# An attention and expert block on one core: the first norm in groups of two tiles, the last attention reordered, and another order in the search of the last batch's entries

## The chip, the core and the metric

The kernel runs on one NeuronCore of a Trainium2 chip. TensorE (PE) multiplies matrices and transposes, VectorE (DVE), ScalarE (ACT) and GpSimd (POOL) work on tiles of 128 partitions, SyncE (SP) issues transfers; GpSimd issues the indirect ones. The engines run side by side, each in the order of its own program, and wait for each other by semaphores that count up. The metric is the device time of one execution in microseconds (us). Three runs of the kernel before took 449.43, 449.25 and 447.59 us; the median is 449.25.

## What is computed

The input x is 4 batches of 512 tokens with 512 features; a context holds 64 rows of 128 for each batch.

```python
x = x + jnp.tanh(g_xattn[0]) * _L0_xattn_ref(_layernorm(x, axis=-1), ctx_512, Wq, Wkv_expand, Wout)
x = x + jnp.tanh(g_ffn[0]) * _L0_ffn_ref(_layernorm(x, axis=-1), gate_w, w1, w2, w3, ws1, ws2, ws3)
# attention: 16 heads of 32, causal mask over the 64 context rows, softmax, Wout
# feed-forward: softmax of 8 gate logits, the top 2 experts of each token with their weights,
#   silu(x w1) * (x w3) w2 for them, plus one shared expert of the same shape for every token
```

## The kernel before, in words

Tokens are worked on in 16 tiles of 128, four to a batch. Every matrix is held as two halves of 16 bits, a high one that ScalarE writes (`hi`, L705) and a low one, the rest, that VectorE writes (`lo`, L1061 and L1062), and each product is three matmuls per pair of halves (`product`, L1671). TensorE's transposes (`turn`, L1676) bring tiles into the layout that a product needs; each is followed by its high and its low half.

The program has these stages on TensorE: the first batch's norm, projections, keys and scores; then for each batch b an `iteration` that finishes its attention while the shared expert ("feed-forward") of batch b-1 runs; for the last batch `last_attention` (b = 3, feed-forward of batch f = 2) and `last_feed_forward` (f = 3); and behind them a loop over 39 expert tiles (`step`): 128 rows of tokens are gathered by an indirect transfer, multiplied with the expert's weights, scaled and added to the output. The loop can begin when the list of entries (which token at which place) is known.

The order of the work is written out by hand, engine by engine; nothing schedules it. The places that the change touches:

- Start. VectorE takes `statistics1` of tiles 0 to 3 (L1098), aggregates (L1105), adds epsilon (L1109); GpSimd raises to the power -0.5 (`power1`, L557); VectorE writes the four norms (`first_norm`, L1093). `LN1_GROUPS` says which tiles share one power. TensorE fills its waits with matmuls of the identity that nobody reads (`keep_clock`, L1970).
- Last attention. `head_sum` (L1183, L1186) gives the softmax's sums to GpSimd, which multiplies (L597); TensorE turns the eight probability tiles; `probabilities_lo` writes their low halves; `attend` (L1813) multiplies probabilities and values for the head groups in the order `ATTEND_LAST`, into the banks `mm_bank[g]`; `project_out` (L1824) follows. The banks 0, 1 and 3 of `mm_bank` hold results of the shared expert's `hidden` and of the router until VectorE has read them, so `attend` waits for `g_ready` and `lg_out`.
- Last feed-forward. `router` gives logits; VectorE takes their maximum away (`router_logits`), chooses two experts in some 15 small dependent operations (`router_choose`) and writes a mask; TensorE counts (`count_pairs`, L1752); VectorE turns the counts into places (`last_place`), and writes one-hot rows and blocks (`rows_hot` L1414, `blocks_hot` L1420 and L1422); ScalarE scales each row twice (`send_lists`, L813, 16 operations); TensorE adds them up (`place_lists`, L1767) and finds the entries (`find_entries`, L1777 to L1781); VectorE writes them (L1462). Around them stand the shared expert's `hidden`, `turn_g`, `down` (a product of six matmuls) and VectorE's `hidden` (L1272, L1275) and `base` (L1282, adds a `down` to x). `down(f - 1, 3)` waits for the base of tile 1, `down(f, 0)` for that of tile 2.

In the listing of `bank` names below, bank0 and bank1 are `score_bank`, bank2 and bank3 `turn_bank`, bank4 to bank7 `mm_bank[0]` to `[3]`.

Of the kernel before, what the change touches and what calls it, by code (L numbers as in the profile page):

```python
# [32 lines left out]
P = 128  # L33
# [39 lines left out]
def block_program(nc, x, ctx_rows, gates, wq, wkv, wout, gate_w, experts, out):  # L73
    with ExitStack() as stack:
# [255 lines left out]
        ATTEND_LAST = (0, 2, 3, 1)  # L330

        def down_bank(f, i):
            if f < B - 2:
                return mm_bank[2 + i % 2]
            return (score_bank[1], mm_bank[2], mm_bank[3], mm_bank[2])[i] if f == B - 2 else mm_bank[3 - i % 2]

# [25 lines left out]
        LN1_GROUPS = ((0, PER), (PER, 2 * PER), (2 * PER, NT))  # L362
# [149 lines left out]
        def _(pool):  # L512
# [53 lines left out]
            power1(0)  # L566

# [50 lines left out]
            def iteration(b, prev):  # L618
# [8 lines left out]
                if prev is None:  # L627
                    power1(2)
# [26 lines left out]
            power1(1)  # L655
# [47 lines left out]
        def _(act):  # L703
# [103 lines left out]
            def send_lists():  # L807

                act.wait_ge(sent_step, 3)
                for g in range(2 * PER):  # L810
# [70 lines left out]
            def last_feed_forward(f):  # L881
# [10 lines left out]
                tanh_h(f, 1)  # L892
                tanh_h(f, 2)
                send_lists()
                tanh_h(f, 3)
                got0_high()
                for i in range(PER):
                    turn_hi(c, "g", i)
# [157 lines left out]
        def _(dve):  # L1056
# [32 lines left out]
            def first_norm():  # L1089

                dve.wait_ge(ln1_power, 1)
                for i in range(PER):
                    V.tensor_scalar(xn1[:, i * D:(i + 1) * D], x_tile(i), ln1[:, i, 0:1], ln1[:, i, 2:3],  # L1093
# [33 lines left out]
            def make_x1(b, i):  # L1127
                t = 4 * b + i
                dve.wait_ge(y_mm, t + 1)
                V.scalar_tensor_tensor(out=x_tile(t), in0=mm_bank[i][:, :], scalar=gl[:, 0:1], in1=x_tile(t),  # L1130
# [24 lines left out]
            dve.wait_ge(ld_x0[0], 16)  # L1155
            statistics1(range(2))
            dve.wait_ge(ld_x0[1], 16)
            statistics1(range(2, PER))
            aggregate1(0)
# [168 lines left out]
            def last_attention(b, f):  # L1328
# [6 lines left out]
                turn_lo(b, "x2", 3)  # L1335
                hidden(f, 1)
                head_sum(b, 1)
                turn_lo(b, "g", 0)
                head_sum(b, 2)
                hidden(f, 2)  # L1340
                head_sum(b, 3)
                router_logits(f)
                for i in range(PER):
                    probabilities_lo(b, i)
                hidden(f, 3)
# [139 lines left out]
            def last_feed_forward(f):  # L1485
# [6 lines left out]
                turn_lo(c, "x2", 3)  # L1492
                turn_lo(f, "g", 2)
                turn_lo(f, "g", 3)
                router_logits(f)
# [5 lines left out]
                base(f - 1, 1)  # L1501
# [3 lines left out]
                listed_before()  # L1505
                add_lists()
                turn_lo(c, "g", 0)
                read_entries()
                read_table()
                base(f - 1, 2)  # L1510
# [24 lines left out]
            def iteration(b, prev):  # L1535
# [22 lines left out]
                if prev is None:  # L1558
                    aggregate1(2)
# [11 lines left out]
                if prev is None:  # L1571
                    bias1(2)
# [20 lines left out]
            aggregate1(1)  # L1593
# [524 lines left out]
```

## Time and profile before

| what | value |
|---|---|
| timed runs, us | 449.43, 449.25, 447.59 |
| the profiled execution's own time | 452.13 us |
| its span, first to last instruction | 450.4 us |
| mean granted TensorE clock | 0.986 |
| busy: PE, DVE, ACT, POOL | 414.9, 306.4, 239.3, 229.6 us |
| the chain that ended last, by engine | PE 61%, DVE 19%, POOL 7%, ACT 6%, issue 4% |
| start to the first projection | 14.55 us |
| last attention and last feed-forward | about 195 to 258 us |
| loop over expert tiles | from about 260 us to the end |

All times within the execution are counted from the start of the span. "Busy" is the time in which an engine had an instruction at work; a matmul's end is modelled. The granted clock is a share of full speed: 1.00 is 2.4 GHz, 0.50 is 1.2 GHz. The chain goes back from the last instruction, at each step to what released it.

### The profile page before, as it was taken

What the parts mean: (1) busy time and instruction counts of PE and PEld (TensorE: products, weight loads), DVE (VectorE), ACT (ScalarE), POOL (GpSimd) and SP (SyncE); (2) the same over time, 40 slices, a digit from 0 to 9 for tenths busy, and PEclk for the clock granted to TensorE, in tenths of its full rate; (3) what the DMA queues carried; (4) which work ended last, traced back from release to release, by engine and by line L of the source; (5) the groups of instructions that cost most, each with busy time, mean ns of one, the idle gap of its engine ahead of it and who ended that gap; (6) DMA issues with size and microseconds to landing.
All of it is one profiled execution on the core that took longest, in us unless ns stands there. A gap on an engine that the chain in (4) does not pass through costs nothing.

```text
span 450.4 us, 8467 instructions
## 1 busy us (share of the span) xinstructions
PE 414.9 (92%) x2833; PEld 231.2 (51%) x2834; DVE 306.4 (68%) x663; ACT 239.3 (53%) x432; POOL 229.6 (51%) x206
## 2 busy tenths in 40 slices
PE   7989788999999999998987899999999999999980
PEld 7565445545546554464543455555555555555540
DVE  5989998888688876897869889844444444444430
ACT  2797784676647766855323448734344343434330
POOL 4019435636266762679343217565554646565422
PEclk9999999999999999998998999999999999999997
DMA  8940001706006075084343789575766666666543
GB/s 301 418 169 2 1 12 59 235 3 233 3 1 234 1 262 185 1 304 149 110 143 109 214 285 260 98 138 99 136 106 126 102 130 103 106 126 120 92 62 47
DMA packets 20769, 59.52 MB, mean 132 GB/s; under 512 B 3521, under 2 KB 3521, under 8 KB 20354
## 3 DMA queue, kind: packets, MB, share of 16 engines
q0 software_dynamic: 9504, 20.55, 25.4%
q1 hardware_dynamic: 11234, 38.56, 24.2%
q8 instruction: 19, 0.31, 0.3%
q14 instruction: 12, 0.10, 0.1%
HBM read 35.93 MB, written 23.17 MB: 131 GB/s over the span
## 4 chain that ended last, share of the span: by engine, by line
PE 61%; DVE 19%; POOL 7%; ACT 6%; issue 4%; another core or an unknown queue 1%; DMA 1%; POOLq 0%; DVEq 0%; ACTq 0%
PE bank L1671 46%; PE bank L1676 9%; DVE arena L1062 4%; POOL arena L590 3%; PE bank L1813 3%; POOL GT L615 2%; ACT arena L705 2%; DVE mv L1098 2%; DVE mx L1183 2%; ACT arena L753 1%; DVE xn L1152 1%; POOL ln L557 1%; PE bank L1824 1%; PE bank L1801 1%; DVE arena L1061 1%
## 5 line engine op out<-in xcount | busy, mean ns | idle before, releaser
L1671 PE MATMUL bank<-arena,GT 128*128 x468 | 107.4, 379 | 0.0
L689 POOL DMA_INDIRECT out<-rows,entry x39 | 62.7, 1609 | 65.9 <-issue 33.3
L1671 PE MATMUL bank<-arena,gT 128*128 (+1 forms) x336 | 80.2, 375 | 2.5 <-DVE x_sb L1282 1.3
L1671 PEld LDWEIGHTS bank<-arena,GT 128*128 128x128 f16 x468 | 45.8, 98 | 46.5
L705 ACT ACTIVATE arena<-bank 128x512 f16<-128x512 f32 (+1 forms) x88 | 48.5, 587 | 25.5 <-PE bank L1671 11.4
L666 POOL DMA_INDIRECT rows<-xrows,entry x39 | 38.9, 998 | 33.1 <-DVE entry L1462 11.3
L1062 DVE SCALAR_TENSOR_TENSOR arena<-bank,arena 128x512 f16<-128x512 f32 (+1 forms) x72 | 44.7, 663 | 12.4 <-ACT arena L705 7.5
L1671 PEld LDWEIGHTS bank<-arena,gT 128*128 128x128 f16 x336 | 32.5, 98 | 38.6 <-issue 3.2
L1061 DVE TENSOR_TENSOR gT<-bank,gT 128x256 f16<-128x256 f32 x55 | 23.0, 420 | 42.7 <-ACT gT L705 42.7
L1036 ACT ACTIVATE rows<-bank,weight 128x512 f32<-128x512 f32 x38 | 26.1, 687 | 38.0 <-PE bank L1671 38.0
L1627 DVE SCALAR_TENSOR_TENSOR uu<-th,bank 128x256 f32<-128x256 f32 x39 | 16.4, 421 | 43.4 <-ACT th L1003 42.8
L1671 PE MATMUL bank<-arena,x2T 128*128 128x512 f16 x192 | 45.5, 388 | 0.4 <-DVE x2T L1061 0.4
L1003 ACT ACTIVATE th<-bank 128x256 f32<-128x256 f32 x39 | 15.0, 384 | 56.0 <-PE bank L1671 54.2
L1824 PE MATMUL bank<-arena 128*128 128x512 f16 x192 | 43.7, 380 | 0.0
L1671 PE MATMUL bank<-arena 128*128 128x512 f16 x192 | 43.6, 379 | 0.0
L590 POOL TENSOR_TENSOR arena<-arena,mx 128x1024 f32<-128x1024 f32 x16 | 30.3, 1903 | 14.3 <-DVE mx L1177 7.2
L597 POOL TENSOR_TENSOR arena<-arena,rd 128x1024 f32<-128x1024 f32 x16 | 30.2, 1902 | 12.1 <-DVE rd L1186 11.9
L557 POOL TENSOR_TENSOR ln<-ln,minus_half 128x2 f32<-128x2 f32 (+2 forms) x11 | 9.4, 855 | 42.3 <-DVE ln L1109 42.0
L1676 PE MATMUL bank<-ident,arena 128*128 128x128 f32 x192 | 26.9, 277 | 3.7 <-DVE arena L1062 3.3
L1671 PEld LDWEIGHTS bank<-arena,x2T 128*128 128x128 f16 x192 | 18.6, 99 | 21.7 <-issue 1.9
L1671 PEld LDWEIGHTS bank<-arena 128*128 128x128 f16 x192 | 18.6, 98 | 20.5 <-DVE arena L1061 0.2
L575 POOL DMA_INDIRECT lists<-pair,slot x24 | 23.7, 987 | 10.6 <-issue 6.2
(177 smaller groups left out, 675.2 us busy)
## 6 DMA issues: line engine op xcount, KB each, us to landing
x_sb<-in_experts SPq DMA_DIRECT2D x9, 768.0 KB, 6.1
rows<-in_experts SPq DMA_DIRECT2D x6, 768.0 KB, 6.3
xrows<-xn SPq DMA_DIRECT2D x16, 256.0 KB
out<-x_sb SPq DMA_DIRECT2D x16, 256.0 KB
image<-GT SPq DMA_DIRECT2D x5, 768.0 KB, 4.2
arena<-image SPq DMA_DIRECT2D x10, 384.0 KB, 4.0
x_sb<-in_x SPq DMA_DIRECT2D x1, 2048.0 KB, 16.8
x_sb<-in_x SPq DMA_DIRECT2D x2, 512.0 KB, 4.0
```

Source lines behind the costliest of these rows:

```text
L575: nc.gpsimd.indirect_dma_start(out=lists[:, :], out_offset=bass.IndirectOffsetOnAxis(ap=slot[:, b % 2, k, i:i + 1], axis=0), in_=pair[:, b ...
L590: nc.gpsimd.tensor_tensor(sv, sv, mx[:, i, :].unsqueeze(2).to_broadcast([P, NH, SK]), ALU.subtract).then_inc(sub_ready, 1)
L597: nc.gpsimd.tensor_tensor(sv, sv, rd[:, i, :].unsqueeze(2).to_broadcast([P, NH, SK]), ALU.mult).then_inc(p_ready, 1)
L666: nc.gpsimd.indirect_dma_start(out=G[:, j % RING, :], out_offset=None, in_=xrows[:, :], in_offset=bass.IndirectOffsetOnAxis(ap=entry[:, 0, ...
L689: nc.gpsimd.indirect_dma_start(out=out, out_offset=bass.IndirectOffsetOnAxis(ap=entry[:, 1, j:j + 1], axis=0), in_=Y[:, j % RING, :], in_o ...
L705: return nc.scalar.activation(dst, src, ACT.Copy, scale=scale)
L1036: nc.scalar.activation(Y[:, s, :], e_y[s][:, :], ACT.Copy, scale=weight[:, bass.ds(j, 1)]).then_inc(ey_ready, 1)
L1061: return V.tensor_tensor(dst, src, high, ALU.subtract)
L1062: return V.scalar_tensor_tensor(out=dst, in0=src, scalar=scale, in1=high, op0=ALU.mult, op1=ALU.subtract)
L1671: last = nc.tensor.matmul(dst, a, b, start=n == 0, stop=n == len(steps) - 1)
L1676: last = nc.tensor.transpose(dst[:, c * P:(c + 1) * P], src[:, c * P:(c + 1) * P], ident[:, :])
L1824: last = nc.tensor.matmul(mm_bank[i][:, :], aTv[:, u, g, i * P:(i + 1) * P], woutv[:, v, g, :], start=n == 0 and u + v == 0, stop=n == NG ...
```

## The change

It has three parts. (1) `LN1_GROUPS` begins with two groups of two tiles, so the first norm has two powers on GpSimd, and VectorE aggregates the first pair ahead of the second pair's statistics; the other groups' numbers go up by one. (2) In the last attention the order of the head groups is 2, 3, 0, 1 instead of 0, 2, 3, 1; VectorE takes two softmax sums earlier and the logits and hidden 2 after the eight low halves; TensorE gets two clock-keeping matmuls in front of the attention; the output projection writes its banks in the new order (`out_bank`). (3) In the last feed-forward `down(f - 1, 2)` stands ahead of the pair counts, and `down(f - 1, 3)` behind the entries; the logits are taken ahead of the low halves of two transposes of the shared expert, the second of which goes behind the reading of the old lists; the base of tile 1 moves behind the entries; ScalarE scales two groups of rows ahead of a tanh, and turns one tile ahead of another.

```diff
--- before.py
+++ after.py
@@ -327,13 +327,17 @@
 
-        ATTEND_LAST = (0, 2, 3, 1)
+        ATTEND_LAST = (2, 3, 0, 1)
 
         def down_bank(f, i):
...
 
+        def out_bank(b, i):
+
+            return mm_bank[ATTEND_LAST[i] if isinstance(b, int) and b == B - 1 else i]
+
         MIX_FIRST = (("q", 0), ("q", 1), ("v", 0), ("q", 2), ("p", 0), ("v", 1), ("q", 3), ("p", 1), ("v", 2),
@@ -359,7 +363,7 @@
 
-        LN1_GROUPS = ((0, PER), (PER, 2 * PER), (2 * PER, NT))
+        LN1_GROUPS = ((0, 2), (2, PER), (PER, 2 * PER), (2 * PER, NT))
 
@@ -564,6 +568,7 @@
             power1(0)
+            power1(1)
 
             def scatter_pairs(b, choices=(0, 1)):
@@ -625,7 +630,7 @@
                 if prev is None:
-                    power1(2)
+                    power1(3)
                 else:
@@ -652,7 +657,7 @@
 
-            power1(1)
+            power1(2)
             softmax_mask(0)
@@ -804,10 +809,10 @@
 
-            def send_lists():
+            def send_lists(g0, g1):
 
                 act.wait_ge(sent_step, 3)
-                for g in range(2 * PER):
+                for g in range(g0, g1):
                     act.wait_ge(row_hot, g + 1)
@@ -890,11 +895,13 @@
                 tanh_h(f, 1)
+                send_lists(0, 2)
                 tanh_h(f, 2)
-                send_lists()
+                send_lists(2, 2 * PER)
+                got0_high()
+                turn_hi(c, "g", 0)
                 tanh_h(f, 3)
-                got0_high()
-                for i in range(PER):
+                for i in range(1, PER):
                     turn_hi(c, "g", i)
...
             def probabilities_hi(b, i):
@@ -1088,8 +1095,8 @@
             def first_norm():
 
-                dve.wait_ge(ln1_power, 1)
                 for i in range(PER):
+                    dve.wait_ge(ln1_power, 1 + i // 2)
                     V.tensor_scalar(xn1[:, i * D:(i + 1) * D], x_tile(i), ln1[:, i, 0:1], ln1[:, i, 2:3],
@@ -1127,7 +1134,7 @@
             def make_x1(b, i):
...
                 dve.wait_ge(y_mm, t + 1)
-                V.scalar_tensor_tensor(out=x_tile(t), in0=mm_bank[i][:, :], scalar=gl[:, 0:1], in1=x_tile(t),
+                V.scalar_tensor_tensor(out=x_tile(t), in0=out_bank(b, i)[:, :], scalar=gl[:, 0:1], in1=x_tile(t),
                                        op0=ALU.mult, op1=ALU.add).then_inc(x1_ready, 1)
...
             def statistics2(b, i):
@@ -1152,11 +1159,10 @@
 
-            dve.wait_ge(ld_x0[0], 16)
-            statistics1(range(2))
-            dve.wait_ge(ld_x0[1], 16)
-            statistics1(range(2, PER))
-            aggregate1(0)
+            for n in range(2):
+                dve.wait_ge(ld_x0[n], 16)
+                statistics1(range(2 * n, 2 * n + 2))
+                aggregate1(n)
             own_block()
@@ -1333,15 +1339,15 @@
                 turn_lo(b, "x2", 3)
+                head_sum(b, 1)
                 hidden(f, 1)
-                head_sum(b, 1)
+                head_sum(b, 2)
                 turn_lo(b, "g", 0)
-                head_sum(b, 2)
-                hidden(f, 2)
                 head_sum(b, 3)
-                router_logits(f)
                 for i in range(PER):
                     probabilities_lo(b, i)
+                router_logits(f)
+                hidden(f, 2)
                 hidden(f, 3)
@@ -1490,23 +1496,23 @@
                 turn_lo(c, "x2", 3)
+                router_logits(f)
                 turn_lo(f, "g", 2)
-                turn_lo(f, "g", 3)
-                router_logits(f)
                 router_choose(f, 0)
...
                 hidden(f, 1)
-                base(f - 1, 1)
                 rows_hot()
...
                 listed_before()
+                turn_lo(f, "g", 3)
                 add_lists()
...
                 read_table()
+                base(f - 1, 1)
                 base(f - 1, 2)
@@ -1556,7 +1562,7 @@
                 if prev is None:
-                    aggregate1(2)
+                    aggregate1(3)
                 for g in range(NG):
@@ -1569,7 +1575,7 @@
                 if prev is None:
-                    bias1(2)
+                    bias1(3)
                 head_max(b + 1, 1)
@@ -1590,9 +1596,9 @@
             statistics1(range(PER + 2, 2 * PER))
-            aggregate1(1)
+            aggregate1(2)
             project_lo(0, 1)
-            bias1(1)
+            bias1(2)
             keys_lo()
@@ -1821,7 +1827,7 @@
                     for u, v in ((0, 0), (0, 1), (1, 0)):
-                        last = nc.tensor.matmul(mm_bank[i][:, :], aTv[:, u, g, i * P:(i + 1) * P], woutv[:, v, g, :],
+                        last = nc.tensor.matmul(out_bank(b, i)[:, :], aTv[:, u, g, i * P:(i + 1) * P], woutv[:, v, g, :],
                                                 start=n == 0 and u + v == 0, stop=n == NG - 1 and u == 1)
@@ -1879,13 +1885,13 @@
                     turn_probabilities(b, i)
-                pe.wait_ge(g_ready, 4 * f + 3)
+                keep_clock(2, mm_bank[2])
                 split_done(b, "p", 2 * PER - 1)
...
                         pe.wait_ge(lg_out, f + 1)
-                    if g == 1:
-                        pe.wait_ge(g_ready, 4 * f + 4)
+                    if g < 2:
+                        pe.wait_ge(g_ready, 4 * f + 3 + g)
                     attend(b, g).then_inc(a_mm, 1)
@@ -1908,15 +1914,15 @@
                 hidden(f, 1)
+                down(f - 1, 2)
                 count_pairs(f)
                 hidden(f, 2)
-                down(f - 1, 2)
+                turn_g(f, 0)
                 hidden(f, 3)
+                place_lists()
+                turn_g(f, 1)
+                find_entries()
                 down(f - 1, 3)
-                place_lists()
-                turn_g(f, 0)
-                find_entries()
-                turn_g(f, 1)
                 down(f, 0)
...
```

VectorE at the start of the program; `mv` and `ln1` are the statistics and what the norm needs of them, `own` belongs to the expert lists. Before:

```order
L1098 BN_STATS mv<-x_sb 128x6 [waits ld_x0_0]
L1098 BN_STATS mv<-x_sb 128x6
L1098 BN_STATS mv<-x_sb 128x6 [waits ld_x0_1]
L1098 BN_STATS mv<-x_sb 128x6
L1105 BN_AGGR ln1<-mv 128x2 [waits ln1_step]
L1105 BN_AGGR ln1<-mv 128x2 x3
L1109 TENSOR_SCALAR ln1<-ln1 128x4 [waits ln1_step]
L1067 TENSOR_REDUCE own<-before_e 128x1 [waits consts]
L1068 CAST along16<-along 128x128
L1070 SCALAR_TENSOR_TENSOR own<-own,down_no 128x1 [waits own_step]
L1093 TENSOR_SCALAR arena<-x_sb,ln1 128x512 [waits ln1_power]
```

And now (the last row stands for the four norms, each with its own wait):

```order
L1105 BN_STATS mv<-x_sb 128x6 [waits ld_x0_0]
L1105 BN_STATS mv<-x_sb 128x6
L1112 BN_AGGR ln1<-mv 128x2 [waits ln1_step]
L1112 BN_AGGR ln1<-mv 128x2
L1116 TENSOR_SCALAR ln1<-ln1 128x2 [waits ln1_step]
L1105 BN_STATS mv<-x_sb 128x6 [waits ld_x0_1]
L1105 BN_STATS mv<-x_sb 128x6
L1112 BN_AGGR ln1<-mv 128x2 [waits ln1_step]
L1112 BN_AGGR ln1<-mv 128x2
L1116 TENSOR_SCALAR ln1<-ln1 128x2 [waits ln1_step]
L1100 TENSOR_SCALAR arena<-x_sb,ln1 128x512 [waits ln1_power] x4
```

The second pair's statistics now stand behind the first pair's scaling, and each pair has its own.

TensorE between the last probability transposes and the output projection of the last attention; rows with `ident,arena` are transposes, those of 32x512 the attention products, bank4 to bank7 are `mm_bank[0]` to `[3]`. Before:

```order
L1676 MATMUL bank2<-ident,arena 128x128 [waits turned_lo]
L1676 MATMUL bank2<-ident,arena 128x128 x3
L1813 MATMUL bank4<-arena 32x512 [waits turned_lo,g_ready]
L1813 MATMUL bank4<-arena 32x512 x11
L1813 MATMUL bank6<-arena 32x512 x12
L1813 MATMUL bank7<-arena 32x512 [waits lg_out]
L1813 MATMUL bank7<-arena 32x512 x11
L1813 MATMUL bank5<-arena 32x512 [waits g_ready]
L1813 MATMUL bank5<-arena 32x512 x11
```

And now:

```order
L1682 MATMUL bank2<-ident,arena 128x128 [waits turned_lo]
L1682 MATMUL bank2<-ident,arena 128x128 x3
L1976 MATMUL bank6<-ident 128x128 x2
L1819 MATMUL bank6<-arena 32x512 [waits turned_lo]
L1819 MATMUL bank6<-arena 32x512 x11
L1819 MATMUL bank7<-arena 32x512 [waits lg_out]
L1819 MATMUL bank7<-arena 32x512 x11
L1819 MATMUL bank4<-arena 32x512 [waits g_ready]
L1819 MATMUL bank4<-arena 32x512 x11
L1819 MATMUL bank5<-arena 32x512 [waits g_ready]
L1819 MATMUL bank5<-arena 32x512 x11
```

Two matmuls of the identity stand ahead of the attention; the bank that waited for nothing new comes first, those of hidden 2 and 3 last.

TensorE in the last feed-forward, from hidden 1 (bank5) to the first down product of the last batch; `mask16` are the pair counts, bank4 and bank5 with `x2T` hidden 2 and 3, `rows` the list products, `pick` the entries. Before:

```order
L1671 MATMUL bank5<-arena,x2T 128x512 [waits turned_lo]
...
L1752 MATMUL bank0<-mask16,earlier 128x32 [waits mask_ready]
...
L1671 MATMUL bank4<-arena,x2T 128x512 [waits g_ready,turned_lo]
...
L1671 MATMUL bank7<-arena,gT 128x512 [waits lg_out,turned_lo]
...
L1671 MATMUL bank5<-arena,x2T 128x512 [waits g_ready,turned_lo]
...
L1671 MATMUL bank6<-arena,gT 128x512 [waits base_ready,turned_lo]
...
L1767 MATMUL bank1<-rows 128x384 [waits sends,hots,base_ready]
L1767 MATMUL bank1<-rows 128x384 [waits sends,hots] x7
L1676 MATMUL bank2<-ident,gg 128x128 [waits turned_lo,g_ready]
...
L1781 MATMUL bank0<-pick,got 128x39 [waits got_ready]
...
L1676 MATMUL bank3<-ident,gg 128x128 [waits turned_lo,g_ready]
...
L1671 MATMUL bank7<-arena,gT 128x512 [waits base_ready,turned_lo]
```

And now:

```order
L1677 MATMUL bank5<-arena,x2T 128x512 [waits turned_lo]
...
L1677 MATMUL bank7<-arena,gT 128x512 [waits lg_out,turned_lo]
...
L1758 MATMUL bank0<-mask16,earlier 128x32 [waits mask_ready]
...
L1677 MATMUL bank4<-arena,x2T 128x512 [waits g_ready,turned_lo]
...
L1682 MATMUL bank2<-ident,gg 128x128 [waits turned_lo,g_ready]
...
L1677 MATMUL bank5<-arena,x2T 128x512 [waits g_ready,turned_lo]
...
L1773 MATMUL bank1<-rows 128x384 [waits sends,hots,base_ready]
L1773 MATMUL bank1<-rows 128x384 [waits sends,hots] x7
L1682 MATMUL bank3<-ident,gg 128x128 [waits turned_lo,g_ready]
...
L1787 MATMUL bank0<-pick,got 128x39 [waits got_ready]
...
L1677 MATMUL bank6<-arena,gT 128x512 [waits base_ready,turned_lo]
...
L1677 MATMUL bank7<-arena,gT 128x512 [waits base_ready,turned_lo]
```

The product into bank7 moved ahead of the counts, that into bank6 from ahead of the list products to behind the entries, and one transpose of `gg` to ahead of hidden 3.

## Rows read from the trace of the kernel before

**Rows 1.** The page: the span.
```profile
span 450.4 us, 8467 instructions
```
**Rows 2.** The chain that ended last: start us, us, what.
```profile
260.49 3.88 PE bank L1671 x18
```
**Rows 3.** Timeline of the start: start us, us, engine, line, what [idle before <-releaser].
```profile
2.38 6.03 PE L1970 MATMUL bank<-ident 128*128 128x128 f32 x28 [2.38 <-POOL earlier L523]
...
4.43 2.54 DVE L1098 BATCH_NORM_STATS2 mv<-x_sb 128x6 f32<-128x512 f32 x4 [4.43 <-DMA x_sb<-in_x]
...
7.12 0.38 DVE L1105 BATCH_NORM_AGGREGATE ln<-mv 128x2 f32<-128x6 f32 x4
7.53 0.17 DVE L1109 TENSOR_SCALAR ln<-ln 128x4 f32<-128x4 f32 x1
...
7.86 1.05 POOL L557 TENSOR_TENSOR ln<-ln,minus_half 128x4 f32<-128x4 f32 x1 [2.58 <-DVE ln L1109]
...
8.95 1.91 DVE L1093 TENSOR_SCALAR arena<-x_sb,ln 128x512 f32<-128x512 f32 x4 [0.85 <-POOL ln L557]
...
14.55 5.35 PE L1671 MATMUL bank<-arena 128*128 128x512 f16 x24
```
**Rows 4.** Timeline, a norm of two tiles in the last attention.
```profile
219.82 0.69 DVE L1098 BATCH_NORM_STATS2 mv<-x_sb 128x6 f32<-128x512 f32 x1
...
221.20 0.72 POOL L557 TENSOR_TENSOR ln<-ln,minus_half 128x2 f32<-128x2 f32 x1 [3.52 <-DVE ln L1109]
```
**Rows 5.** Timeline of the last attention, up to its products.
```profile
199.93 5.74 POOL L597 TENSOR_TENSOR arena<-arena,rd 128x1024 f32<-128x1024 f32 x3 [1.01 <-DVE rd L1186]
...
203.65 3.41 PE L1676 MATMUL bank<-ident,arena 128*128 128x128 f32 x24
...
203.87 4.86 DVE L1062 SCALAR_TENSOR_TENSOR arena<-bank,arena 128x512 f16<-128x512 f32 x8
204.28 3.41 ACT L705 ACTIVATE arena<-bank 128x512 f16<-128x512 f32 x6
```
**Rows 6.** Attention products: the timeline; stretches: us, PE busy (x), others, PEclk.
```profile
57.55 2.77 PE L1813 MATMUL bank<-arena 64*32 64x512 f16 x48 [1.73 <-DVE arena L1062]
...
208.88 4.46 PE L1813 MATMUL bank<-arena 64*32 64x512 f16 x48 [1.83 <-DVE arena L1062]
...
208.88:213.34 4.46, 4.46 (x49) 1.97 (x50) 2.15 (x5) 1.79 (x3) 4.30 (x6) 0.62 0.58 180
...
171.75:174.45 2.70, 2.70 (x51) 1.14 (x52) 1.95 (x3) 2.38 (x4) 0.00 (x0) 1.00 0.61 170
```
**Rows 7.** Timeline of the last feed-forward, around the router's logits.
```profile
233.86 0.65 PE L1671 MATMUL bank<-gate_s,x2T 128*128 128x8 f16 x20
...
234.96 0.66 ACT L705 ACTIVATE gT<-bank 128x256 f16<-128x256 f32 x2 [3.76 <-remote]
...
236.05 0.18 DVE L1198 TENSOR_REDUCE m<-bank 128x4 f32<-128x32 f32 x1
```
**Rows 8.** Timeline, TensorE around the mask.
```profile
235.02 2.75 PE L1671 MATMUL bank<-arena,x2T 128*128 128x512 f16 x12
...
240.31 0.21 PE L1752 MATMUL bank<-mask,earlier 128*128 128x32 f16 x1 [2.54 <-DVE mask L1236]
...
240.55 4.18 PE L1671 MATMUL bank<-arena,x2T 128*128 128x512 f16 x12
```
**Rows 9.** Timeline of the search, up to the loop's first product.
```profile
243.02 0.74 DVE L1282 SCALAR_TENSOR_TENSOR x_sb<-bank,gl,x_sb 128x512 f32<-128x512 f32 x1
...
245.04 4.77 ACT L813 ACTIVATE rows<-rows,sent 128x128 f16<-128x128 f16 x16
...
249.74 1.46 PE L1767 MATMUL bank<-rows 128*128 128x384 f16 x8
...
252.22 0.19 DVE L1462 TENSOR_SCALAR entry<-bank 128x39 int32<-128x39 f32 x1
...
260.32 2.75 PE L1671 MATMUL bank<-arena,GT 128*128 x12
```

## The prediction

> **What bounds the kernel now.** I read the chain that ended last first, then the timelines of the three places that the change touches, then a table of stretches for the granted clock. From 260.49 us on the chain is TensorE alone, one expert tile after another [rows 2]; no edit touches that loop, so the time changes only by how much earlier or later it begins. Before it the three places bound differently.
>
> At the start VectorE sets the end: 28 clock-keeping matmuls end at 8.41, the four statistics are done at 6.97, aggregation and scaling at 7.70, GpSimd's power ends at 8.91, and only then VectorE writes the norms, without a pause until the first projection at 14.55 [rows 3]. In the last attention VectorE is full too: eight low halves of the turned probabilities from 203.87 to 208.73, and TensorE, which ended its transposes at 207.06, waits 1.83 us for them [rows 5, 6]. In the last feed-forward TensorE waits 2.54 us for the router's mask (VectorE's chain of small operations) before the pair counts [rows 8]; then the search for the entries runs over VectorE, ScalarE and TensorE in turn and ends at 252.22 + 0.19; the loop's first product starts at 260.32 [rows 9].
>
> Two things in this execution need care. First, the granted clock. After the wait of 1.83 us the attention's 48 matmuls take 4.46 us with the mean clock at 0.62, where the same 48 take 2.70 at 1.00 [rows 6]: 1.76 us lost to the lower level (1.2 GHz instead of 2.4). After the wait of 2.54 the twelve matmuls of a hidden product take 4.18 instead of 2.75: 1.43 us [rows 8]. A wait of 1.73 elsewhere cost nothing: 48 matmuls in 2.77 [rows 6]. Second, ScalarE stands still for 3.76 us before 234.96 with "remote" as its releaser, although the transposes that it needed had been issued well before [rows 7]; the router's logits on VectorE, queued behind it, start at 236.05. Without it they would follow TensorE's router products. Those had issued 20 of 24 matmuls in 0.65 us from 233.86 [rows 7], so the whole lasts 0.78 and the logits start some 0.13 later, at 234.77: 1.28 us earlier. The mask's wait then shrinks to 1.7 us, for TensorE is earlier too (0.47 us, its own pause at 234.5), and a wait of 1.73 kept the clock. An execution without the standstill is thus shorter by 1.28 + 1.43 = 2.71.
>
> **The time that the sum starts from.** The profiled execution took 452.13 us, 1.73 around its span of 450.40 [rows 1]. Minus 2.71 that is 449.42; the timed runs are 449.43, 449.25 and 447.59. So I take the timed runs to have no standstill, two of them one fall of the clock, and the third none: it is 1.66 to 1.84 below, and the fall costs 1.76. Start: 449.42.
>
> **Part 1, the first norm in groups of two.** The first pair's statistics end 1.27 after 4.43, the aggregation for two and its scaling end at about 6.3, the second pair's statistics at 7.5, its scaling at 8.1 and the three small "own block" operations at 8.45. From last statistics to the start of a power for two columns it is 0.69 us (220.51 to 221.20), and the power lasts 0.72 [rows 4], against 1.05 for four [rows 3]; the first power then ends at 7.1 and the second at 8.9, before norm 2 needs it at 9.35. Norm 0 starts at 8.42 instead of 8.95: -0.53. TensorE's next two keeping matmuls now follow the 28 directly and end at 9.0, when norm 0 is there. Behind it VectorE is full until 14.55, so the gain goes through. Bounds: 0 (TensorE's dummies or a weight split is late) and -0.9 (the whole pause in front of norm 0). Added: one power (0.72, GpSimd idle), one more aggregation group on VectorE (0.3, in its pause).
>
> **Part 2, the last attention.** Sum 1 moves ahead of hidden 1, and the logits and hidden 2 behind the eight low halves; the first of these can start at 202.8 instead of 203.87. But from the third on they follow ScalarE's high halves, six in 3.41 us from 204.28 [rows 5], and TensorE's transposes, which come behind a hidden product that does not move. The eighth low half of VectorE then starts at 207.98 at best and ends at 208.6: -0.13. The softmax's third multiply on GpSimd ends 0.5 earlier [rows 5], which nobody waits for. The logits and hidden 2 and 3 (0.4 + 0.8 + 0.8) now stand between 208.5 and 210.5, inside the attention products: product 3 of the new order 2, 3, 0, 1 needs hidden 2 at 211.0 and gets it at 209.6. The two keeping matmuls (0.6) run in the wait and leave 1.1 us idle in place of 1.83; with 1.73 kept, the clock stays: -1.76. Bounds: 0 (it falls all the same) and -1.76. I take -1.76.
>
> The Trainium skill ("TensorE: Matmul & The Clock Gate", "What's actually happening") says that what watches TensorE runs free and does not restart with a kernel, so that the same wait may be followed by a fall in one execution and not in another. The trace cannot show it, but the third timed run agrees; by that rule the medians before hold either 447.6 or 449.3, and the gain of this part is 1.76 or nothing.
>
> **Part 3, the search.** Three effects. (a) The base of tile 1 (0.74, [rows 9]) leaves VectorE's path in front of the hot rows, a low half (0.34) enters it before the lists are added, and ScalarE's 16 scaled copies, 4.77 us in one run [rows 9], can start with the first hot rows: entries 0.43 earlier. (b) That base and TensorE's down product of tile 3 (half of a hidden product's 2.75, 1.3 issued) now stand behind the entries. There both engines have no pause to speak of: 8.1 us from the entries' write to the first loop product [rows 9]. All but 0.2 of the 1.3 is new there: +1.10. Sum of (a) and (b): +0.67. Bounds: -0.43 (all of (b) hidden) and +1.3. The down product of tile 2, put in the mask's wait, is hidden there (1.3 into 1.7), but what it filled before it no longer fills. (c) That is the clock. Before, hidden 3 and two down products kept TensorE full until the eight list products, which ran back to back in 1.46 us [rows 9]. Now hidden 3 ends at 244.9, and the list products come one by one behind ScalarE's copies until 247.3; then TensorE waits for the fourth low half, the entries and the moved base. Its work from 244.9 to 250.2 is 1.46 + 0.4 + 0.4 + 0.2 = 2.5 us, 2.9 idle in pieces. After 1.83 idle in one piece the clock fell, so I expect a fall here. A fall costs 1.43 to 1.76 where TensorE is always busy; some 0.4 of slack are left, I take +1.2. Bounds 0 and +1.76.
>
> **Sum.** 449.42 - 0.53 - 0.13 - 1.76 + 0.67 + 1.2 = 448.87; forecast 448.9, no change that can be told from 449.25. What a measurement here can tell is about 0.5%, 2.2 us.
>
> **Rivals.**
> - R1, no fall in the emptied stretch. For it: TensorE never idles 1.8 in one piece there. Against: half of the stretch is idle. 448.87 - 1.2 = 447.7. Chance 0.18.
> - R2, the standstill at 231.2 belongs to the program and every run has it. For it: its releaser is a real event, and the work of all engines stops on it. Against: the sum above meets the timed runs only without it. Then the logits move ahead of the two low halves that wait for ScalarE and gain 0.77, the second fall (1.43) goes, since the wait shrinks by the product put in it, and the new fall comes: part 3 gives 0.67 - 0.77 - 1.43 + 1.2 = -0.33, and the timed 449.25 becomes 449.25 - 0.53 - 0.13 - 1.76 - 0.33 = 446.5. Chance 0.24. [...]
> - R3, slower: the clock falls in the last attention in spite of two keeping matmuls (0.6 of 1.8 us filled, and the low level lasts through all four products), while part 3 costs its full price. 449.42 - 0.53 - 0.13 + 0.67 + 1.2 = 450.6, and 451.2 if part 1 is hidden. It decides as soon as TensorE's remaining idle of 1.1 us counts as the 1.83 did. Chance 0.12.
> - That the change does not move what it says is excluded for part 1 and 3 by the order of instructions; others, 0.04.
>
> **Range and chances.** Forecast 0.42 (447.9 to 449.7), R1 0.18 (446.8 to 448.4), R2 0.24 (445.4 to 447.4), R3 0.12 (449.9 to 452). 446.0 to 450.7 leaves out half of R3's upper part and the lower third of R2. Faster by over 0.5% (below 447.0): 0.20 of R2, 0.06 of R1, 0.02 else: 0.28. Slower (above 451.5): 0.04 of R3, 0.02 else: 0.06. The rest, 0.66.
>
> **What would show it.** Norm 0 near 8.4 and the first projection near 14.0. The attention's 48 matmuls in 2.7 to 2.8 at a clock of 1.00, with the eighth low half ending near where it did, counted from hidden 3. No ScalarE wait for "remote" of 3.8 us (else R2). TensorE waiting 0.6 for the mask. From the entries' write to the first loop product 9.0 us or more, with the clock down in between; if it is under 8.3 at full clock, part 3 was priced wrongly.

## The result, and the profile after

The changed kernel takes 450.16 us, the median of 20 runs (447.47 to 452.46); the kernel before, run beside it, 448.33 (447.38 to 450.63, 20 runs). The ratio is 1.0039, 95% interval 1.0024 to 1.0054: slower, by less than the 0.5% that the prediction called no change. The forecast of 448.9 had the sign wrong; 450.16 lies inside the range and outside the likeliest case's own (447.9 to 449.7).

The single times stand at levels. For the changed kernel the mean granted clock of the run is given in brackets, and it goes with them:

| kernel | us (mean clock where given), number of runs |
|---|---|
| before, 20 runs | 447.4 to 447.6, 10; 449.1 to 449.5, 9; 450.63, 1 |
| changed, 20 runs | 447.5 (0.993), 1; 449.0 to 449.4 (0.988 to 0.99), 6; 450.1 to 450.4 (0.984), 7; 451.7 to 452.5 (0.98), 6 |

The profiled execution of the changed kernel took 451.73, 1.73 around its span. The start, in the timeline, answers to [rows 3]:

```profile
6.23 1.28 DVE L1105 BATCH_NORM_STATS2 mv<-x_sb 128x6 f32<-128x512 f32 x2
...
8.41 1.91 DVE L1100 TENSOR_SCALAR arena<-x_sb,ln 128x512 f32<-128x512 f32 x4
9.00 1.11 PE L1682 MATMUL bank<-ident,arena 128*128 128x128 f32 x8 [1.04 <-DVE arena L1100]
...
14.00 1.25 PE L1677 MATMUL bank<-arena 128*128 128x512 f16 x5
```

Norm 0 starts at 8.41 and the first projection at 14.00, as forecast. Attention products and the search answer to [rows 6] and [rows 9]:

```profile
57.02 4.15 PE L1819 MATMUL bank<-arena 64*32 64x512 f16 x48 [1.73 <-DVE arena L1069]
...
207.62 0.61 PE L1976 MATMUL bank<-ident 128*128 128x128 f32 x4
209.51 0.83 PE L1819 MATMUL bank<-arena 64*32 64x512 f16 x12 [1.29 <-DVE arena L1069]
...
242.33 3.60 ACT L818 ACTIVATE rows<-rows,sent 128x128 f16<-128x128 f16 x12
...
245.49 0.32 PE L1773 MATMUL bank<-rows 128*128 128x384 f16 x1 [0.26 <-ACT rows L818]
...
246.07 0.32 PE L1773 MATMUL bank<-rows 128*128 128x384 f16 x1 [0.26 <-ACT rows L818]
...
247.14 0.41 PE L1682 MATMUL bank<-ident,gg 128*128 128x128 f32 x2 [0.75 <-DVE gT L1068]
...
247.94 0.20 DVE L1468 TENSOR_SCALAR entry<-bank 128x39 int32<-128x39 f32 x1
...
248.26 1.39 DVE L1288 SCALAR_TENSOR_TENSOR x_sb<-bank,gl,x_sb 128x512 f32<-128x512 f32 x2
...
249.14 5.28 PE L1677 MATMUL bank<-arena,gT 128*128 128x512 f16 x12 [1.24 <-DVE x_sb L1288]
...
254.53 1.46 PE L1677 MATMUL bank<-arena,gT 128*128 128x512 f16 x6
...
259.74 2.54 PE L1677 MATMUL bank<-arena,GT 128*128 x11
```

Stretches of the same trace (us, busy time and count of TensorE, its weight loads, VectorE, ScalarE and GpSimd, then granted clock, DMA share, GB/s):

```profile
56.43:59.84 3.41, 2.83 (x28) 1.07 (x32) 2.63 (x12) 1.62 (x3) 1.20 (x1) 0.50 0.00 0
...
209.51:212.28 2.77, 2.77 (x49) 1.18 (x50) 2.67 (x8) 2.02 (x4) 2.77 (x4) 1.00 0.64 162
...
243.46:249.14 5.68, 2.87 (x16) 1.16 (x15) 5.35 (x26) 3.71 (x13) 0.08 (x1) 0.86 0.73 294
247.58:254.41 6.83, 5.59 (x18) 2.24 (x17) 4.38 (x15) 0.38 (x1) 2.90 (x3) 0.50 0.59 174
```

Three things are to be seen. The last attention keeps its clock (2.77 us at 1.00, where [rows 6] has 4.46 at 0.62). The first attention, whose code the change leaves alone, has lost it behind a wait of 1.73 us: 4.15 us, while the same wait in [rows 6] was followed by 2.77. And in the search TensorE is busy for only 2.87 us of the 5.68 from the first list product to the two down products; after these short pieces of work, with waits of 0.26, 0.75 and 1.24 us between them, the clock is down for 6.83 us, so that the twelve matmuls of the two down products take 5.28 (2.75 at full clock in e5, below). From the entries to the loop's first product it is 259.74 - 247.94 = 11.80 us (8.10 in [rows 9]). The mask's wait and ScalarE's:

```profile
231.11 0.38 ACT L710 ACTIVATE gT<-bank 128x256 f16<-128x256 f32 x1 [0.96 <-PE bank L1682]
...
237.85 0.19 PE L1758 MATMUL bank<-mask,earlier 128*128 128x32 f16 x1 [0.39 <-DVE mask L1242]
```

No standstill of 3.76 us [rows 7], and 0.39 for the mask in place of 2.54 [rows 8]; the prediction's sign was 0.6.

### The profile page after: what moved, and what is told of

It reads as the page before. It is cut to its first block, busy times and chain, and to the rows that moved or that the text cites. A ratio compares the mean times of both kernels' runs of the same rounds, so it can differ in the third digit from the quotient of the medians.

```text
span 450.0 us, 8478 instructions
## 1 busy us (share of the span) xinstructions
PE 415.2 (92%) x2837; PEld 230.4 (51%) x2838; DVE 306.5 (68%) x664; ACT 239.4 (53%) x432; POOL 228.0 (51%) x207
## 4 chain that ended last, share of the span: by engine, by line
PE 65%; DVE 15%; ACT 6%; POOL 6%; issue 4%; DMA 1%; POOLq 0%; DVEq 0%; ACTq 0%
PE bank L1677 50%; PE bank L1682 10%; DVE arena L1069 4%; PE bank L1819 3%; POOL GT L620 2%; ACT arena L710 2%; POOL arena L595 2%; DVE mv L1105 2%; ACT arena L758 1%; DVE xn L1159 1%; PE bank L1830 1%; PE bank L1807 1%; ACT rows L818 1%; POOL ln L561 1%; DVE arena L1068 1%
## 5 line engine op out<-in xcount | busy, mean ns | idle before, releaser
L694 POOL DMA_INDIRECT out<-rows,entry x39 | 61.5, 1578 | 69.4 <-issue 34.2
L1677 PE MATMUL bank<-arena,gT 128*128 (+1 forms) x336 | 82.6, 384 | 2.6 <-DVE x_sb L1288 1.6
L1677 PE MATMUL bank<-arena,x2T 128*128 128x512 f16 x192 | 44.0, 379 | 0.4 <-DVE x2T L1068 0.4
L1068 DVE TENSOR_TENSOR GT<-bank,GT 128x512 f16<-128x512 f32 x39 | 26.9, 690 | 2.8 <-ACT GT L710 0.8
```

What stands on the lines that cost most here:

```text
L694: nc.gpsimd.indirect_dma_start(out=out, out_offset=bass.IndirectOffsetOnAxis(ap=entry[:, 1, j:j + 1], axis=0), in_=Y[:, j % RING, :], in_o ...
L1068: return V.tensor_tensor(dst, src, high, ALU.subtract)
L1677: last = nc.tensor.matmul(dst, a, b, start=n == 0, stop=n == len(steps) - 1)
```

## The experiments

Five jobs; in each the kernels run in turns with the kernel before on one chip. "Keeping matmuls" are `keep_clock`, each about 0.3 us, on a bank that nobody uses then. "Kept" is a place whose wait has them. The prices below are taken inside one job, or between jobs 2 and 3, which ran on one chip; any other difference across jobs is rougher.

**Job 1, the parts alone** (before here: 447.7, 13 runs; 449.3, 15; 450.71, 1). e1 is the norm's edits, e2 the last attention's with its two keeping matmuls, e3 the search's, e4 e1 and e2 together: each a part of the diff above, word for word.

> Only the first norm in groups of two (part 1). All theories: norm 0 at 8.4 and first projection at 14.0 as in the changed kernel, 0.53 us less where TensorE's clock does the same. Theory S (the search order and the clock falls in its emptied stretch are the whole loss): the runs lie 0.5 below those of the kernel before, at about 447.0 and 448.8, median near 448. Rival N (the shift by 0.55 us is what brings the clock down in the first attention, 57 us, where the changed kernel's profile has it): a level 1.4 higher appears, median 449 or more.

> Only the last attention's new order and the two clock-keeping matmuls (part 2). Theory S: the upper of the two levels of the kernel before (449.3 against 447.5) thins out or goes, because the fall in the last attention does, and both are 0.1 lower: most runs near 447.4, median 447.4 to 447.8. Rival A (the keeping matmuls don't hold the clock in other executions, or the fall of the timed runs is elsewhere, at the mask's wait): two levels as before, median 448.3 to 449.2.

> Only the search's new order (part 3). Theory S: no run under 448.0 (447.4 + 0.67), most at 450 to 452: one or two falls of 1.3 to 2.7 us on top, median about 451, slower than before by 2 to 3 us. Rivals N and A: the search is worth what its order gives, 0.67 at most, median 448.5 to 449.3. The profile should show 11 to 12 us from the entries' write to the loop's first product and the clock at 0.50 in it.

> Parts 1 and 2 with the search as before. Theory S: 0.66 below the kernel before at equal clock, and the last attention's fall gone: most runs at 446.8, some one fall higher (448.5), median 446.8 to 447.5, faster than before by 1 us or more. Rival N: a third of the runs or more at 448.2 and above because of the first attention; median 448.5. Rival A: two levels at 446.9 and 448.6 in equal numbers.

Measured: e1 447.10 (447.0 in 7 runs, 448.5 to 448.8 in 4, one 450.15). e2 448.79 (447.2 in 4, 449.1 in 8). e3 452.43, ratio 1.0081 (1.0052 to 1.0110), no run under 449.99. e4 448.31, ratio 0.9977 (0.9959 to 0.9995): 447.0 in 5, 448.4 in 7. So the search is the loss, and parts 1 and 2 are a gain of 0.7 us between the lower levels (447.0 against 447.7). In the profile of e3's fastest run (449.99) it is 257.94 - 247.38 = 10.56 us from the entries to the loop, not the 11 to 12 expected, with one fall of the clock. The timeline, then the stretch:

```profile
248.58 4.09 PE L1673 MATMUL bank<-arena,gT 128*128 128x512 f16 x12 [1.24 <-DVE x_sb L1284]
...
247.94:251.35 3.41, 2.77 (x7) 1.02 (x8) 2.25 (x6) 0.00 (x0) 2.24 (x3) 0.50 0.61 192
```

But the second level did not go with the last attention's fall: rival A's two levels came in e2 and e4, though not from the mask's wait that it named. The profiles of both show where the fall was, at the first attention. Since e2 has it without part 1, rival N (part 1's shift brings it) is not needed. Of e4:

```profile
57.00 4.26 PE L1817 MATMUL bank<-arena 64*32 64x512 f16 x48 [1.73 <-DVE arena L1067]
...
209.56 2.77 PE L1817 MATMUL bank<-arena 64*32 64x512 f16 x48 [1.29 <-DVE arena L1067]
```

**Job 2.** e5 keeps the clock in the search's emptied stretch:

```
...
                                             start=g == 0, stop=g == 2 * PER - 1)
+                    if 4 <= g < 7:
+                        keep_clock(1, score_bank[0])
...
+                pe.wait_ge(pos_out, B)
                 place_lists()
+                keep_clock(3, score_bank[0])
                 turn_g(f, 1)
                 find_entries()
+                keep_clock(4, score_bank[1])
                 down(f - 1, 3)
```

e6 undoes the moved work:

```
                 hidden(f, 1)
+                base(f - 1, 1)
                 rows_hot()
...
                 read_table()
-                base(f - 1, 1)
...
                 hidden(f, 3)
+                down(f - 1, 3)
                 place_lists()
                 turn_g(f, 1)
                 find_entries()
-                down(f - 1, 3)
```

e7 is e4, and e8 the kernel before, with four keeping matmuls in the first attention (e8: four in the last attention too):

```
+if prev is None:
+    pe.wait_ge(v_lo, 1)
+    keep_clock(4, mm_bank[0])
 split_done(b, "p", 2 * PER - 1)
```

> The changed kernel with ten more clock-keeping matmuls in the stretch that its search empties: one behind each of list products 5 to 7, three ahead of the turn of g 1, four (1.2 us) ahead of the down product that waits for the base. Theory S (the falls in that stretch are what makes the changed kernel slower; the moved work costs about 0.6 at full clock): the levels with mean clock 0.984 and 0.980 go, what is left are runs at 447.5 and, with one fall elsewhere, 449.1; median 447.5 to 449.1, at or under the kernel before. Rival W (the moved base and down product themselves cost it, the clock only follows): median stays at 450 or above.

> The changed kernel with two things put back: down product 3 of the batch before stands ahead of the list products again, and its base 1 on VectorE ahead of the hot rows. The rest of the search's new order stays. Theory S: the emptied stretch is full again; the copies of ScalarE still start early, so the entries come about as early as in the kernel before or a little earlier. Levels 446.6 to 447.0 and one fall higher (448.4 to 448.7); median 447 to 448.5. Rival P (what hurts is the single copies and list products, which still arrive one by one): the clock still falls there, median 449 or more.

> Parts 1 and 2 (search as before) and four clock-keeping matmuls (1.2 us) in the wait of 1.73 us in front of the first attention's products at 57 us. Theory F (the second level of the runs is one fall of the clock at that wait): the level at 448.4 goes, all runs at 446.9 to 447.1. Rival M (the fall of the other runs is in the wait for the router's mask, 1.7 us at 235 us, or anywhere else): two levels as in the kernel with parts 1 and 2, 447.0 and 448.4, median between.

> The kernel before with four clock-keeping matmuls (1.2 us) in each of two waits, in front of the first attention's products (1.73 us) and of the last attention's (1.83 us), nothing else changed. Theory F: all runs at 447.4 to 447.7, the level at 449.3 is gone. Rival M: two levels, 447.5 and 449.3, as before. If only some of the upper level goes, both waits and a third place share the falls.

Measured: e5 447.78, ratio 0.9988 (0.9969 to 1.0006): nine runs at 447.6 to 448.3, three at 449.1 to 449.7. Only ten idle-time matmuls and one wait (`pos_out`) away from the changed kernel, it is 2.4 us below the first comparison's 450.16, and the ratio to the kernel before is 0.9988 against 1.0039; W falls. From its entries to the loop it is 257.33 - 248.11 = 9.22 us at full clock.

```profile
248.11 0.20 DVE L1468 TENSOR_SCALAR entry<-bank 128x39 int32<-128x39 f32 x1
...
249.31 2.75 PE L1677 MATMUL bank<-arena,gT 128*128 128x512 f16 x12 [0.25 <-DVE x_sb L1288]
...
257.33 2.75 PE L1677 MATMUL bank<-arena,GT 128*128 x12
```

e7 446.86, ratio 0.9961 (0.9948 to 0.9975), and e8 447.54, ratio 0.9974 (0.9959 to 0.9990): 12 runs each, one level each. Theory F holds: the two levels of the kernel before are falls of the clock at these two waits. A third level, 450.4 to 451.2, holds 12 of its 138 runs outside job 4; it is gone too, and its height fits both falls in one run, but no profile shows it. The wait for the mask, 1.69 us, stays unfilled in e7 and e8, and no run of theirs stands on an upper level. e6 451.65 (six runs, 451.4 to 453.4, ratio 1.0073): S is missed, and P's "449 or more" came by a wait that neither named. I had left the low half of g 3 where the change put it, behind the hot rows, and the down product needs it.

```profile
248.15 2.27 PE L1677 MATMUL bank<-arena,gT 128*128 128x512 f16 x6 [4.09 <-DVE gT L1068]
```

**Job 3.** e9 is the changed kernel with the four of e7. e10 is e6 with them and with `turn_lo(f, "g", 3)` ahead of VectorE's hidden 1. e11 is e7 without part 2's `keep_clock(2, mm_bank[2])`. e12 is e1 with the keeping matmuls of e8.

> The changed kernel with four clock-keeping matmuls in the wait of 1.73 us in front of the first attention's products, nothing in the search. Theory S: what is left are the falls in the emptied stretch, of 3.4 us (cost 1.5) or 6.8 us (cost 2.7); levels 447.5 (rare), 449.0 and 450.2, the one at 451.9 gone; median 449.0 to 450.2, slower than the kernel with parts 1 and 2 and the same four by 2 to 3 us. Rival: the four also cure the rest, median 447.6.

> The kernel with down product 3 and base 1 put back, with the low half of g 3 put back too (behind the router's choice, ahead of hidden 1), since the down product needs it, and with the four keeping matmuls in the first attention. ScalarE's early copies and down product 2 in the mask's wait remain of the search's new order. Theory L (the loss of the kernel without this was that low half behind the hot rows, for which TensorE stood 4.09 us): the list products follow the down product at once, no wait over 1 us; one level at 446.3 to 447.0, at or below 446.86 of parts 1 and 2 with the four. Rival P (single copies and list products are the trouble): 448 or more, clock down near 247.

> Parts 1 and 2 with the four keeping matmuls in the first attention, but without part 2's own two in the last attention (the wait there is 1.8 us again). If those two keep the clock (theory F): a second level at about 448.5 comes back, in a quarter to a half of the runs. Rival (part 2's order alone, or chance, held it): one level at 446.9 as with them.

> Part 1 and four keeping matmuls in each of the two attention waits; the last attention's order and the search as in the kernel before. It prices part 2's order alone against 446.86 (parts 1 and 2 with the keeping matmuls): by my sum the order is worth 0.13, so 447.0; if it is worth nothing, 446.9; if it is worth more, 447.2. And against the keeping matmuls alone (447.54) it prices part 1: 0.53 gives 447.0, one level.

Measured: e9 450.20: 447.69 once, 448.7 to 449.4 three times, 450.1 to 450.6 (clock 0.984) eight times; the level at 452 is gone. So the changed kernel's levels are, by their height and clock: no fall, a short or a long one in the stretch, and the long one with the first attention's. Profiles show the long one (e9) and the last (the changed kernel). e10 448.18: L is right that the wait of 4.09 goes (the longest left is 1.24, not under 1), the four runs at full clock lie at 447.0 to 447.4, but in eight the time is 447.9 to 449.3, and the profile of one has the clock down for 6.83 us, as P had it: it takes full clock to judge an order. e11 446.97: nine runs at 446.7 to 447.0, three at 448.4 to 448.9, so without part 2's two matmuls a second level is back in 3 of 12. That these are falls in the last attention is inferred: e11's profile is of a run without one, and only [rows 6] shows that fall. e12 447.05, one level.

**Job 4** ran on a chip where the kernel before takes 448.97 in 5 runs and 450.4 to 453.7 in 12. e13 is e5 with the four of e7; e14 is e10 with a keeping matmul behind list products 6 and 7 and four behind the entries; e15 is e7 again.

> The changed kernel with the clock kept everywhere: four keeping matmuls in the first attention's wait, ten in the search's emptied stretch, the last attention's two as they are. Theory S: one level, at 447.6 to 447.8, no run above 448.3; minus 446.86 it is what the search's new order costs at full clock, 0.8. Rival W (part of the loss of the changed kernel is neither the order nor the clock): a second level or a median above 448.3.

> The kernel with the down product, base 1 and low half of g 3 put back and the first attention kept, with six keeping matmuls more in the search: one behind each of list products 6 and 7, four ahead of the down product that waits for the base. Theory S: one level at 446.9 to 447.3 (its lower level without them was 447.2), all of the upper one was the clock. If ScalarE's early copies and down product 2 in the mask's wait are worth anything, it is below 446.86; I expect not.

> Parts 1 and 2 with the four keeping matmuls in the first attention, once more, beside the two others on the same chip: one level, 446.8 to 447.1, and the fastest of the three.

Measured: e13 448.25 and e14 447.72, six runs and one level each; e15 449.14, six runs at 448.1 and six at 449.9, ratio 0.9970 (0.9949 to 0.9991). The expected numbers are missed by 0.4 to 2.0 us; the reason is in all three profiles. Of e15:

```profile
232.32 0.66 ACT L710 ACTIVATE gT<-bank 128x256 f16<-128x256 f32 x2 [3.74 <-remote]
...
237.66 0.19 PE L1756 MATMUL bank<-mask,earlier 128*128 128x32 f16 x1 [2.53 <-DVE mask L1240]
```

This is the standstill of [rows 7] with the mask's wait of [rows 8]. No profile of the other jobs has it. So it goes with this chip or this job, which one job cannot tell apart, and it is in the timed runs too: 448.97 is 1.5 above the 447.5 of other jobs, the prediction's price of it 1.28. Which chip the profile of the kernel before came from is not on record.

**Job 5**, on a chip without it (before 447.5 in 11 runs, 449.1 in 13, 450.5 in 2). e16 is e7 with `keep_clock(4, score_bank[0])` ahead of `count_pairs(f)` in the last feed-forward, behind a wait for `pos_out`; e17 is e14, e18 the changed kernel.

> Parts 1 and 2, four keeping matmuls in the first attention, and four more (1.2 us) in TensorE's wait for the router's mask (1.7 us, or 2.5 where ScalarE stands still for 3.8 us). If the second level of the same kernel without the last four, 1.8 above the first on the chip with the standstill, is a fall at that wait: one level here on either kind of chip, 446.9 without the standstill, 448.1 with it. Rival: it comes from elsewhere, two levels 1.8 apart remain on a chip with the standstill.

> The kernel e14 again, beside the others. With the standstill 447.7 as before, and 0.2 to 0.5 faster than the one with the mask's wait kept, since the router's logits come ahead of the low half that waits for ScalarE; without it 447.0 to 447.2, not faster than it.

> The changed kernel as it is. Without the standstill: levels 447.6, 449.1, 450.2, 452, median 450.2, beside 448.3 to 449.2 of the kernel before. With the standstill, where the search's new order wins some of it back: 448.3 at full clock, mostly 449.8 to 451.5, median near the 450.5 that the kernel before has there.

Measured: e16 446.62, ratio 0.9956 (0.9939 to 0.9973), one level; e17 446.97, one level; e18 451.62, ratio 1.0046 (1.0023 to 1.0069), seven of its twelve runs at 451.6 to 452.6. For e18 the expected median, 450.2, is missed by 1.4: more of its runs stand on the highest level than in the first comparison (7 of 12, there 6 of 20). That the mask's wait makes e15's second level is not shown, since e16 did not meet the standstill and e15's profile has no fall; for it speak [rows 8], where the clock fell behind that wait of 2.54, and e13 and e14, which wait 0.49 and 0.48 there and have no second level. How the changed kernel does on that chip stays open too. e16 has the lowest median of the study, 2.3 us under the kernel before and 0.35 under e17 beside it; against e7 and e12, from other jobs, it is not told apart.

## Why the prediction was wrong

By its own terms, with what the runs gave. Levels are compared at the same clock; jobs 2 and 3 were on one chip.

| term | predicted | measured |
|---|---|---|
| part 1 | -0.53 | -0.49 (e12 447.05 less e8 447.54) |
| part 2, order | -0.13 | -0.19 (e7 446.86 less e12 447.05) |
| part 2, clock | -1.76 in the median | -0.5 on average (e11's mean 447.37 less 446.89, e7's) |
| part 3, (a) and (b) | +0.67 | +0.9 (e5's lower level 447.74 less e7) |
| part 3, (c) clock | +1.2 | +2.0 on average (e9's mean 449.79 less 447.74) |

**What held.** Part 1 came through behind its full VectorE. The 1.7 us that it worked out for the mask's wait without the standstill are 1.69 in e1, e2, e4, e7, e8, e11 and e12. At full clock the three orders nearly cancel: 447.5 before, 447.5 in the changed kernel's one undisturbed run and 447.64 in e18's. "From the entries' write to the first loop product 9.0 us or more" is 9.22 in e5, 8.10 + 1.10 plus 0.02. The timed runs had no standstill (their lower level is 1.5 us under job 4's), and part 2's matmuls kept the clock wherever a profile shows the last attention with them.

**The step that failed first** is the term -1.76 of part 2, which measured -0.5. It rests on the start, "two of them one fall of the clock", with the fall taken to be the last attention's, because the profile had it there. The wait of 1.73 us in the first attention "cost nothing" in that one execution [rows 6] and so left the sum. In fact either wait may lose the clock. With the last attention kept and the first not (e2, e4) 15 of 24 runs are on the upper level; with the first kept and the last not (e11) 3 of 12. So part 2 took away the smaller share, 0.5 us on average, and left the larger. The prediction had worked out, from the Trainium skill ("TensorE: Matmul & The Clock Gate", "What's actually happening"), where what watches TensorE runs free and does not restart with a kernel, that the same wait may be followed by a fall in one execution and not in another. These counts agree with that. It would have told against -1.76: I used it for the wait that had fallen and not for the one that had not.

**The second** is the size of (c). A fall in the emptied stretch was forecast, but at +1.2, the price of one low stretch with 0.4 of slack. Only three of e9's twelve runs pay about that (448.7 to 449.4). Eight are at 450.1 to 450.6, 2.4 to 2.9 above its undisturbed run; in the profile of one of them, as in that of the changed kernel, the clock stays down twice as long as in e3's:

```profile
245.72:252.55 6.83, 5.53 (x18) 2.15 (x19) 4.88 (x16) 0.38 (x1) 2.89 (x3) 0.50 0.59 190
```

In e5 the ten matmuls leave TensorE 0.5 us idle in 5.65, where the changed kernel has 2.8 in 5.68, and the clock is whole:

```profile
243.66:249.31 5.65, 5.14 (x37) 3.62 (x36) 5.37 (x26) 3.72 (x13) 0.09 (x1) 1.00 0.71 278
```

The order's price, (a) and (b), was 0.2 too low: in the profiles of e5 and e7 the entries come 0.4 us earlier, counted from the last attention, as forecast, but from the entries to the loop it is 9.22 against 7.94 (8.11 in e8), so (b) is 1.1 to 1.3 where 1.10 was taken.

With the measured averages the sum is -0.49 - 0.19 - 0.5 + 0.9 + 2.0 = +1.7; the means of the 20 and 20 runs differ by 450.30 - 448.47 = 1.83.

**Luck.** The terms of the change together missed by 2.3 us (+1.7 against -0.55), the time only by 1.3 (450.16 against 448.87). The rest is mostly the start: 449.42 was the upper level that two of three runs showed, and the median of 20 is 448.33. That 450.16 lies inside the range is owed to this.

**The rivals.** R1 (no fall in the stretch) is one run of twelve in e9. R3 gave a time close to the measured, 450.6, and half of its mechanism: part 3 cost its full price and more, but the last attention, where it put the other fall, kept its clock; the first lost it. R2's premise is true of job 4's chip in that job and false for the others; its time was for all. In job 4 the search's order costs 448.25 (e13) less 448.1 (e15's lower level), 0.2 us where elsewhere it costs 0.9, which is the direction R2 gave (0.67 - 0.77).

## What to carry to other kernels

A wait of TensorE that one profile shows without a fall of the clock is not proven free: test every wait of that size (of three here, 1.73 and 1.83 us lost the clock in some runs, and 1.69 in none of the 36 of e7, e8 and e12), and read the levels of many timed runs and their mean clocks before one of them is credited with the difference. Work that is moved out of the critical path may have been what kept the clock; here 0.9 us of order became 2.9 with the clock, and a handful of idle-time matmuls gave it back. Compare orders at full clock first (keep it in every long wait), since otherwise the clock's luck hides differences of 0.2 to 0.9 us.

## What the runs showed that I had not expected

Where a trace has the clock down it is down for 3.41 us, as in both attentions, or for 6.83, as in the search of the changed kernel, e9, e10 and e18. Short pieces of work with waits of 0.26 to 1.24 us between them were enough: one such stretch was followed by 3.41 in e3 and by 6.83 in the changed kernel, with the same waits, so the waits alone do not decide which. Filling the wait of 1.73 us to 0.84 was enough in every run: no run of e7, e8, e12, e16 and e17 (57 in all) stands on a level of its own 1.5 us up. And a standstill of ScalarE of 3.7 to 3.8 us can stay with a chip or a job, whatever the kernel: it is at the same instruction in all three profiles of job 4 and in that of the kernel before, and absent in the sixteen others of this study. What makes it is open.
